# ScalarE takes the projected rows out of PSUM, GpSimd adds x and multiplies two masks

## The reference

```python
h = _layernorm(x, axis=-1) * (1 + ca) + sa
x = x + ga * _L0_attn_ref(h, ...)      # 16 heads of 16, softmax over 1024 keys, output projection, bias
h = _layernorm(x, axis=-1) * (1 + cb) + sb
x = x + gb * _L0_ffn_ref(h, ...)       # 32 experts, each row goes to 6, and a shared expert
# routing in _L0_ffn_ref
scores = jax.nn.sigmoid(logits)
sfc = scores + e_score_correction_bias[None, :]
group_scores = sfc.reshape(T, N_GROUP, gs).max(axis=-1)
_, gidx = jax.lax.top_k(group_scores, TOPK_GROUP)       # 4 of 8 groups
...
masked = jnp.where(smask, sfc, 0.0)
_, topk_idx = jax.lax.top_k(masked, TOP_K)              # 6 of 32 experts
tw = jnp.take_along_axis(scores, topk_idx, axis=1)
tw = tw / (tw.sum(-1, keepdims=True) + 1e-20)
```

## Time and profile before

| | us |
|---|---|
| median of 3 runs | 1427.59 (1424.33 to 1433.63) |
| the profiled execution's own time | 1430.49 |
| its span, first to last instruction | 1428.7 |
| PE busy in the span | 1359.2 (95%) |
| DVE busy | 1129.7 (79%) |
| ACT busy | 754.5 (53%) |
| POOL busy | 606.7 (42%) |

### The profile page before, as it was taken

How to read it: one execution, slowest core, us unless ns; L and a number is a source line. 1 busy time by engine, 2 the same in 40 slices (tenths; PEclk the granted TensorE clock), 3 DMA queues, 4 the chain that set the end, 5 groups by cost and what they waited for, 6 DMA issues and landing times.

```text
span 1428.7 us, 30863 instructions
## 1 busy us (share of the span) xinstructions
PE 1359.2 (95%) x8207; PEld 677.6 (47%) x8208; DVE 1129.7 (79%) x2815; ACT 754.5 (53%) x1155; POOL 606.7 (42%) x782
## 2 busy tenths in 40 slices
PE   7997999999999999999999999989999999999996
PEld 3552223332333323333333233558788888887552
DVE  7886999999999999999999992656566666665477
ACT  3772577667666767676667677113333333333100
POOL 4000113233744725546346366327755555555200
PEclk9997799999999999999999999999999999999998
DMA  6887355534346435454465346837766656555788
GB/s 213 273 266 201 102 165 134 112 91 106 99 127 166 103 101 140 124 135 101 112 162 146 80 134 198 257 124 237 226 202 203 203 168 189 180 173 173 270 304 317
DMA packets 216960, 243.55 MB, mean 170 GB/s; under 512 B 93949, under 2 KB 181501, under 8 KB 216738
## 3 DMA queue, kind: packets, MB, share of 16 engines
q1 hardware_dynamic: 189330, 166.42, 42.8%
q0 software_dynamic: 21776, 68.07, 13.4%
q10 hardware_dynamic: 5760, 7.87, 1.7%
HBM read 133.98 MB, written 108.28 MB: 170 GB/s over the span
## 4 chain that ended last, share of the span: by engine, by line
PE 68%; DVE 14%; DMA 5%; issue 2%; SPq 1%; ACT 1%; POOL 0%; DVEq 0%; POOLq 0%
PE psO L1171 14%; PE ex_psGU L1670 13%; PE psE L1158 13%; PE psM L1148 9%; DVE piece_max L1046 9%; PE ex_psY L1685 6%; PE ex_psX L1661 3%; PE psM L505 2%; PE co_psS L1935 2%; PE ex_psA L1679 2%; DMA wide<-results 1%; DMA results<-vals_inv,places 1%; PE psGU L1486 1%; PE late_psGU L1915 1%; PE psM L524 1%
## 5 line engine op out<-in xcount | busy, mean ns | idle before, releaser
L1046 DVE TENSOR_REDUCE piece_max<-psM 128x1 f32<-128x512 f32 x1024 | 642.2, 681 | 28.6 <-PE psM L1148 25.3
L1112 ACT ACTIVATE wide<-psE 128x1024 f32<-128x1024 f32 x512 | 497.1, 1021 | 208.4 <-PE psE L1158 206.2
L1148 PE MATMUL psM<-wide 48*128 48x512 bf16 x1024 | 324.5, 396 | 20.4 <-DVE piece_max L1046 12.0
L1158 PE MATMUL psE<-wide 49*128 49x512 bf16 (+1 forms) x2048 | 331.0, 382 | 2.4 <-DMA wide<-maxima 2.4
L1752 POOL DMA_INDIRECT results<-vals_inv,places x223 | 213.9, 959 | 155.9 <-DVE vals_inv L1738 89.9
L1171 PE MATMUL psO<-wide 128*32 128x512 f32 x2048 | 275.4, 610 | 0.6 <-ACT wide L1112 0.6
L1148 PEld LDWEIGHTS psM<-wide 48*128 48x128 bf16 x1024 | 78.2, 93 | 348.4 <-DVE piece_max L1046 275.8
L1670 PE MATMUL ex_psGU<-wide,ex_xT 128*128 x892 | 233.0, 384 | 0.6 <-ACT ex_xT L1703 0.6
L1158 PEld LDWEIGHTS psE<-wide 49*128 49x128 bf16 (+1 forms) x2048 | 117.9, 95 | 94.0 <-issue 10.4
L1670 PEld LDWEIGHTS ex_psGU<-wide,ex_xT 128*128 128x128 f32 x892 | 153.1, 192 | 15.6 <-issue 2.9
L1703 ACT ACTIVATE ex_xT<-ex_psX 128x256 f32<-128x256 f32 x223 | 85.6, 384 | 123.7 <-PE ex_psX L1661 122.5
(11 more groups left out here) (280 smaller groups left out, 1271.8 us busy)
## 6 DMA issues: line engine op xcount, KB each, us to landing
wide<-qk_parts SPq DMA_DIRECT2D x384, 64.0 KB
wide<-results SPq DMA_DIRECT2D x16, 1536.0 KB, 8.6
rows<-lists SPq DMA_DIRECT2D x112, 160.0 KB
h2Ts<-lists SPq DMA_DIRECT2D x111, 160.0 KB
qk_parts<-parts SPq DMA_DIRECT2D x32, 384.0 KB, 3.0
xin<-in_x_dram SPq DMA_DIRECT2D x16, 512.0 KB, 4.0
v_values<-vst SPq DMA_DIRECT2D x32, 256.0 KB, 3.6
wide<-v_values SPq DMA_DIRECT2D x16, 512.0 KB
```

What stands on the lines that cost most here:

```text
L1046: v.tensor_reduce(piece_max[:, qh, (x * PAIRS + h) * KT // QH + qt, kh:kh + 1], bank_of("piece", PIECES * group + n), AX.X, ALU.max, negat ...
L1112: nc.scalar.activation(probs[:, step % 2, 2 * pair:2 * pair + 2], psE[:, pair], ACT.Exp, scale=HD ** -0.5).then_inc(exp_ok, 1)
L1148: nc.tensor.matmul(bank_of(*user), qa[g][rows, h, qt * P:(qt + 1) * P], ka[g][rows, h, kh * 512:(kh + 1) * 512], start=True, stop=True).th ...
L1158: mm = nc.tensor.matmul(psE[:, pair, x], k[g][part, pair, kt * P:(kt + 1) * P], q[g][part, pair, qh * 512:(qh + 1) * 512], start=(q is qa) ...
```

## The change

Four things change, all for the seven chunks that are routed beside attention.

1. The projected rows leave PSUM by a new ACT copy (`projected_out`) behind the second exponential of steps 12 and 13, and POOL adds x to them in SBUF (`add_x`, two additions of 128x512). PE's piece that takes over the bank waits for the copy. The four statistics move from slots 50, 51, 54 and 55 to slots 57 to 60.
2. The mask of the groups (`masked`) and the choice of scores (`chosen`) are multiplied by POOL, the first as four instructions of 128x32.
3. The maxima of two halves are joined by a reduction over adjacent pairs in place of a two-operand minimum.
4. Transposes, gate and places run one step later, and the routing from slot 100 runs four slots later (`PICK`). On POOL the additions of x stand before the first portion of scatters, and the masks before the third.

```diff
--- before.py
+++ after.py
@@ -53,7 +53,8 @@
 WINDOW = 2 * STEPS
 DIVIDE = 5
 VALUES = 38
-PROJECT, TURN, GATE, PLACE = 11, 21, 23, 28
+PROJECT, TURN, GATE, PLACE = 11, 22, 24, 29
+STATS, PICK = 57, 104
 PORTIONS = (0, 11, 15, 19, 24)
 KEYS = 8
 LOWEST = -3.0e38
@@ -553,6 +554,20 @@
     act.wait_ge(env.gated, c + 1)
     wait(act, env.sc_ok, c)
     env.nc.scalar.activation(env.bent[:], of[:, 0:TPC * E], ACT.Tanh, scale=0.5).then_inc(env.bent_ok, 1)
+
+
+def statistics(dve, env, c, i):
+
+    if i % 2 == 0:
+        dve.wait_ge(env.x2_ok, 2 * c + i // 2 + 1)
+    env.nc.vector.bn_stats(env.stats[:, i], env.x2[:, TPC * c + i]).then_inc(env.stats_ok, 1)
+
+
+def projected_out(act, env, c, half, of):
+
+    act.wait_ge(env.projected, 2 * c + half + 1)
+    env.nc.scalar.activation(env.x2[:, TPC * c + 2 * half:TPC * c + 2 * half + 2], of.rearrange("p (i d) -> p i d", i=2),
+                             ACT.Copy).then_inc(env.copied, 1)
 
 
 def route_part(dve, env, chain, c, d, of):
@@ -663,14 +678,23 @@
         then(strike(env.gmax, env.gkeys, env.gleft))
     elif d == 106:
         ready()
-        then(v.tensor_tensor(env.gmask[:], env.gmax[:, :, 0:GROUPS], env.gleft[:, :, 0:GROUPS], ALU.not_equal))
+        mask = v.tensor_tensor(env.gmask[:], env.gmax[:, :, 0:GROUPS], env.gleft[:, :, 0:GROUPS], ALU.not_equal)
+        if c < LAST:
+            mask.then_inc(env.groups_masked, 1)
+        else:
+            then(mask)
+    elif d == 107 and c < LAST:
+        pass
     elif d == 107:
         ready()
         then(v.tensor_tensor(env.masked[:, :, 0:E].rearrange("p i (g k) -> p i g k", g=GROUPS),
                              env.sfc[:].rearrange("p i (g k) -> p i g k", g=GROUPS),
                              bc(env.gmask[:].unsqueeze(3), TPC, GROUPS, EPG), ALU.mult))
     elif d == 108:
-        ready()
+        if c < LAST:
+            dve.wait_ge(env.masked_ok, c + 1)
+        else:
+            ready()
         then(largest(env.masked, E))
     elif d == 109:
         ready()
@@ -683,11 +707,16 @@
         v.tensor_tensor(env.sel[:], env.masked[:, :, 0:E], env.unmasked[:, :, 0:E], ALU.not_equal).then_inc(env.sel_ok, 1)
     elif d == 112:
         dve.wait_ge(env.sel_ok, c + 1)
-        v.tensor_tensor_scan(env.rank[:].rearrange("p i e -> p (i e)"), env.ones[:, 0:TPC * E],
-                             env.sel[:].rearrange("p i e -> p (i e)"), 0.0, ALU.mult, ALU.add)
-        then(v.tensor_tensor(env.chosen[:], env.sc[:], env.sel[:], ALU.mult))
+        scan = v.tensor_tensor_scan(env.rank[:].rearrange("p i e -> p (i e)"), env.ones[:, 0:TPC * E],
+                                    env.sel[:].rearrange("p i e -> p (i e)"), 0.0, ALU.mult, ALU.add)
+        if c < LAST:
+            then(scan)
+        else:
+            then(v.tensor_tensor(env.chosen[:], env.sc[:], env.sel[:], ALU.mult))
     elif d == 113:
         ready()
+        if c < LAST:
+            dve.wait_ge(env.chosen_ok, c + 1)
         then(v.tensor_reduce(env.wsum[:], env.chosen[:], AX.X, ALU.add))
     elif d == 114:
         ready()
@@ -934,6 +963,24 @@
                 pool.wait_ge(env.vals_in, 16 * VALS_LOADS * (c + 1))
                 g.tensor_tensor(env.vals[:], env.vals[:], env.inv[:], ALU.mult).then_inc(env.vals_ok, 1)
 
+            def add_x(c):
+                for half in range(2):
+                    pool.wait_ge(env.copied, 2 * c + half + 1)
+                    x2 = env.x2[:, TPC * c + 2 * half:TPC * c + 2 * half + 2]
+                    g.tensor_tensor(x2, x2, env.xin[:, 2 * half:2 * half + 2], ALU.add).then_inc(env.x2_ok, 1)
+
+            def mask_groups(c):
+                pool.wait_ge(env.groups_masked, c + 1)
+                for i in range(TPC):
+                    ins = g.tensor_tensor(env.masked[:, i, 0:E].rearrange("p (g k) -> p g k", g=GROUPS),
+                                          env.sfc[:, i].rearrange("p (g k) -> p g k", g=GROUPS),
+                                          env.gmask[:, i].unsqueeze(2).to_broadcast([P, GROUPS, EPG]), ALU.mult)
+                ins.then_inc(env.masked_ok, 1)
+
+            def weigh_experts(c):
+                pool.wait_ge(env.sel_ok, c + 1)
+                g.tensor_tensor(env.chosen[:], env.sc[:], env.sel[:], ALU.mult).then_inc(env.chosen_ok, 1)
+
             def inverse_deviations(c):
                 pool.wait_ge(env.stats_ok, TPC * (c + 1))
                 even, odd = env.stats[:, :, 1], env.stats[:, :, 4]
@@ -1015,6 +1062,7 @@
             add_bias(0)
             for c in range(LAST):
                 multiply_values(c)
+                add_x(c)
                 scatter_portion(c - 1, 1)
                 inverse_deviations(c)
                 normalise(c)
@@ -1026,6 +1074,8 @@
                     add_bias(c + 1)
                     scatter_portion(c - 1, 2)
                 scores(c)
+                mask_groups(c)
+                weigh_experts(c)
                 scatter_portion(c - 1, 3)
                 weights_and_places(c)
                 if c < LAST - 1:
@@ -1050,7 +1100,7 @@
                 part = piece_max[:, k % QH]
                 cols = slice(COLS * (k % QH), COLS * (k % QH + 1))
                 dve.wait_ge(piece_read, HALF_PIECES * (k + 1))
-                chain.link(v.tensor_tensor(neg_max[:, cols], part[:, :, 0], part[:, :, 1], ALU.min))
+                chain.link(v.tensor_reduce(neg_max[:, cols], part, AX.X, ALU.min))
                 wait(dve, max_stored, 4 * 16 * k)
                 v.transpose(neg_max_t[:], neg_max[:]).then_inc(max_ready, 1)
 
@@ -1067,7 +1117,11 @@
                     if w == 0 and n == 0 and c == 0:
                         dve.wait_ge(env.consts, CONSTS)
                         dve.wait_ge(const_in, 16 * 6)
-                    route_part(dve, env, steps, c, 4 * w + n, bank_of(c, w - 1))
+                    slot = 4 * w + n
+                    if STATS <= slot < STATS + TPC:
+                        statistics(dve, env, c, slot - STATS)
+                    elif slot == VALUES or slot >= PICK:
+                        route_part(dve, env, steps, c, slot - PICK + 100 if slot >= PICK else slot, bank_of(c, w - 1))
 
             v.memset(neg_max[:], 0.0).then_inc(env.zeroed, 1)
             for n in range(HALF_PIECES):
@@ -1099,6 +1153,8 @@
 
             def beside(step, pair):
                 c, w = chunk_at(step)
+                if c >= 0 and pair == 1 and w in (PROJECT + 1, PROJECT + 2):
+                    projected_out(act, env, c, w - PROJECT - 1, bank_of(c, w - 1))
                 if c >= 0 and pair == 1 and w in (TURN, TURN + 1):
                     turned_out(act, env, c, w - TURN, bank_of(c, w))
                 if c >= 0 and pair == 1 and w == GATE:
@@ -1130,7 +1186,7 @@
                 if c == "piece":
                     pe.wait_ge(piece_read, w + 1)
                 elif w in (PROJECT, PROJECT + 1):
-                    pe.wait_ge(env.x2_ok, 2 * c + w - PROJECT + 1)
+                    pe.wait_ge(env.copied, 2 * c + w - PROJECT + 1)
                 elif w in (TURN, TURN + 1):
                     pe.wait_ge(env.h2T_ok, KC * c + w - TURN + 1)
                 elif w == GATE:
...
```

More of the change, by code:

```diff
@@ L2051, in declare_routing @@
      env.placed, env.placed_read, env.routed, env.consts, env.zeroed, env.pool_chain, env.dve_chain, env.gu_in,
-     env.down_in, env.pads_known, env.pads_out, env.table_out, env.sfc_ok, env.wrec_ok, env.slot_ok, env.slot_read) = (
+     env.down_in, env.pads_known, env.pads_out, env.table_out, env.sfc_ok, env.wrec_ok, env.slot_ok, env.slot_read,
+     env.copied, env.groups_masked, env.masked_ok, env.chosen_ok) = (
         env.sem("rt_" + n) for n in (
@@ L2056, in declare_routing @@
         "routed", "consts", "zeroed", "pool_chain", "dve_chain", "gu_in", "down_in", "pads_known", "pads_out",
-        "table_out", "sfc_ok", "wrec_ok", "slot_ok", "slot_read"))
+        "table_out", "sfc_ok", "wrec_ok", "slot_ok", "slot_read", "copied", "groups_masked", "masked_ok", "chosen_ok"))
     env.h2T_of = lambda c: env.h2T[:] if c < LAST else env.xin[:].rearrange("p i d -> p (i d)").rearrange("p (k t) -> p k t", k=KC)
```

## The result

| | before | after |
|---|---|---|
| median of 5 runs, us | 1427.59 (1423.52 to 1433.63) | 1448.72 (1443.83 to 1460.06) |
| ratio | | 1.0156 [1.0119, 1.0192] |

The kernel is slower by 21.1 us, where 18.6 were forecast; 1448.7 lies in the range of 1435 to 1458. The profiled execution is the longest of the five, 1460.06. The changed kernel was timed once more beside the experiments, on the chip with number 6: 1445.71 against 1425.73.

The account below looks back on a forecast made before the run. PE was taken to bound plain attention steps, with DVE only 0.09 us behind, and DVE the routing stretch. Six windows at 2.30 us plus 4.8 for the last made 18.6, so 1427.59 + 18.6 = 1446.2 us, range 1435 to 1458.

Parts of the forecast that it names:

- The copy, 0.95 twice: Steps 12 and 13: PE's third piece waits for ACT's copy behind the exponentials, 0.95 us each, 1.90 a window.
- The statistics, 0.93: Steps 14 and 15: all four statistics there make DVE the bound, 0.93 us more a window, bounds 0.5 and 1.46.
- The masks, -0.38: DVE-bound routing stretch: two mask multiplications leave DVE, saving 0.20 and 0.18 us a window.
- The bound of 0.77: Upper bound for DVE's wait on POOL's `masked`, if each of four multiplications takes 0.455 us; two reductions cover 1.20.
- The moved guests, -0.15: First transpose, no longer after the step with `divide`, loses less waiting for a bank: 0.15 us gained, between 0 and 0.3.
- 2.30: Forecast growth in us of each of six windows: 1.90 + 0.93 - 0.38 - 0.15.
- The joined maxima, 0: Joining the maxima by one operation of about 0.17 us changes nothing, or 0.05 either way.
- the rival in which POOL holds DVE's two-operand instructions: DVE's two-operand instructions meet POOL's new operations, or POOL comes too late: 14 us in all, 1460; chance 0.06.
- POOL's slack: POOL's chain ends 2.7 us before the first transpose needs it, and 1.8 us idle remain before the scores.
- The last window, +4.8: Gate product behind the wait for the maxima costs 1.97 us (bounds 1.3 and 2.6); with 1.90 and 0.93, 4.8.
- this rival: PE's new pauses bring a lower clock into each window: 7 x 2.4 = 17 us added, 1463; chance 0.07.
- The sum: Whole kernel: six windows make 13.8 us, the last 4.8, together 18.6, so a median of 1446.2.

Follow-up runs that it names:

- The masks alone: The kernel before with only the two multiplications of masks moved to POOL; 1424.02 us on chip 6, ratio 0.9977.
- guests at their old steps: The changed kernel with transposes, gate, places and routing slots at the steps of the kernel before; 1581.53 and 1584.50 us on chip 14.
- all put back: The changed kernel with ACT's copy before the exponentials, statistics in slots 52 to 55, transposes, gate, places and routing at old steps; 1567.92 us on chip 14.
- early copy and early statistics: The changed kernel with ACT's copy ahead of the next step's exponentials and statistics in slots 52, 53, 57 and 58; 1433.94 us on chip 6.
- the early copy: The changed kernel with ACT's copy ahead of the next step's exponentials; 1437.27 us on chip 6, 1583.96 us on chip 14.
- two statistics early: The changed kernel with the first two statistics in slots 52 and 53, the last two in 59 and 60; 1597.66 us on chip 14.
- masks back on DVE: The changed kernel with both multiplications of masks on DVE again, one instruction each; 1592.82 us on chip 14, ratio 1.0261.
- guests later: The kernel before with only transposes, gate and places one step later and routing four slots later; 1551.73 us on chip 14, ratio 1.0018.
- the join alone: The kernel before with only the maxima joined by a reduction over pairs; 1547.49 us on chip 14, ratio 0.9991.

## Why the prediction was right, and where its size was off

**The copy, 0.95 twice: right.** Measured 0.95 and 0.94. The third piece was released by ACT's copy both times, and moving the copy ahead of the exponentials, nothing else, took both waits away.

**The statistics, 0.93: right.** Measured 0.86 and 0.03. Two of the four put into time in which DVE waits for PE give back 0.5 to 0.6.

**The masks, -0.38: right**, a little small. The masks alone gave 0.46 in a window, and taking them away cost 0.41. The bound of 0.77 for a wait on POOL didn't come to be: I had estimated 1.0 us for POOL's four multiplications, and they took 0.84.

**The moved guests, -0.15: wrong by its size, which is zero.** I had given the first transpose a gain because it no longer follows the step with `divide`. Before, steps 21 to 25 took 16.6 us together, and after 3.20, 3.36, 3.10, 4.52 and 2.30, 16.5; steps 21 to 31 take 35.38 with the guests at their old steps and 35.44 at the new ones. As I read it, the debt of DVE after `divide` is paid by whoever comes next: a guest moved out of its way leaves the same number of reductions to be done. This is most of the difference between 2.30 and the measured 2.4 to 2.5 a window.

**The joined maxima, 0: right,** by the run with it alone. Against the rival in which POOL holds DVE's two-operand instructions stand the steps: the 2.4 us of a window are accounted for without it, and with the copy and the statistics put back (all put back, window 0) only 0.09 in step 14 is left over, though POOL's additions and multiplications are all there. The rule of "SBUF — State Buffer" in the Trainium skill (SBUF: two separate sides) that the two exclude each other could be seen in the join alone at most as the 0.25 us of all 32 joins; the medians differ by 0.1 us, with an interval from 5.0 won to 2.3 lost, so that run can't decide on so little.

**POOL's slack: right to the tenth.** 2.7 us before the first transpose, 1.8 idle at the scores.

**The last window, +4.8: the mechanism was right and the size was off**, 7.3 and 7.0 measured. Its parts 1.90 and 0.93 came, 2.8 over steps 11 to 20. The gate behind the wait for the maxima was to cost 1.97 and cost 4.5 and 4.1. The term held the gate's time at full clock, 1.97, and PE ran it and its neighbours at half clock: 1.65 more for the gate, some 0.87 more for each of three neighbours, and a part of that for a fourth. Before, half clock had lasted there for two products (1.94 in the earlier trace rows's neighbour at 867.14, and 1.59, where 1.06 and 1.04 are their times at full clock). In the kernel with early copy and early statistics, which kept its clock there, the ten steps from 21 on took 26.09, against 26.03 before: at full clock the gate's new place costs about what half clock cost before. Set against the kernel before without its 1.4 us of half clock, the gate's new place costs 1.5, by this estimate, which is within the bounds of 1.3 and 2.6. "TensorE: Matmul & The Clock Gate" (Part 1) in the Trainium skill says that the clock falls when PE has been idle. Of the eight traces with the later gate six agree: after waits of 1.65 and 1.88 us (the changed kernel), 1.83 and 2.74 (the early copy on chip 6 and on chip 14), 1.55 (two statistics early) and 2.56 (masks back on DVE) the gate took 3.62. Two stayed at 2.4 GHz after 2.06 (early copy and statistics) and 2.28 (guests later). So this rival, to which I had given 0.07 for all windows, came true in one place and not in the windows' steps 12 and 13, where PE waited 0.88 twice.

**The sum.** Six times 2.45 and 7.0 to 7.3 are 21.7 to 22.0, against 21.1 and 20.0 of the medians. Taken apart by experiments it closes in the steps and not in the medians: with the copy and two statistics put back the windows are those of before, but the median is still 8.2 us over it.

**Open.** What lets PE keep its full clock over a wait of 2.28 us in one trace and not over one of 1.55 in another. What stops DVE and ACT on the one chip, and what takes 93 us more there behind the windows. Where some 5 us of the kernel with early copy and early statistics go on chip 6. Whether the kernel with everything put back is better than the masks alone: on chip 6, where it could be told, it did not run.

## What to carry to other kernels

Work that is moved to an idle engine costs what its place in that engine's queue costs: a reader that frees a bank stands ahead of the engine's long instructions, not behind them, or the bank's next user pays for them. Only operations taken from the engine that is the bound at that place bring time, here two small masks; additions that DVE did while it waited for PE brought none. A product that stood in a wait for nothing is paid when it is moved behind that wait, and most of its price can be the clock: 4.1 and 4.5 us here where PE fell to half clock behind the wait, and next to nothing over before where it did not. And a few microseconds won on one chip may not be won on another: on chip 14 the variants of the change lost 20 to 48 us where those of chip 6 lost 8 to 20.

## What was not expected of the hardware

- Two chips of the same kind gave 1426 and 1548 us for the same kernel. In a kernel traced on both, window 0 takes the same time to 0.06 us. Of the 120 us that the kernel with the join alone takes more than the kernel before on the other chip, 27 lie in the windows, in stops of DVE and ACT of up to 4 us beside POOL's scatters, and 93 behind them.
- POOL multiplies four times 128x32 in 0.84 us, where 128x4 takes 0.20 and 128x128 0.455.
- In the same order of work, PE's clock fell to 1.2 GHz for the gate product (3.62 us) in six traces and stayed at 2.4 GHz (1.97 us) in two others. The length of the wait ahead of it doesn't tell which: it fell after 1.55 to 1.88, 2.56 and 2.74 us, and stayed after 2.06 and 2.28.
